# TensorE's attention as a loop with a register count over pairs of token blocks, with two V slots, x normalised by ScalarE and transposed two blocks at a time

## The reference

```python
xn = rms_norm(x)                                  # x * rsqrt(mean(x*x) + 1e-6)
qkv = xn @ w_qkv.T                                # w_qkv: 3072 x 128
q, k, v = split, 16 heads of 64
q, k = apply_rope(q, cos, sin), apply_rope(k, cos, sin)
attn = where(0 <= q_pos - k_pos <= 32, q @ k.T / 8, -1e9)
out = softmax(attn) @ v
y = out @ w_out.T                                 # back to 128 channels
```

## Time and profile before

| | us |
|---|---|
| median of 3 runs | 500.16 |
| lowest, highest | 496.52, 503.5 |
| the profiled execution's own time | 501.18 |
| its span | 499.3 |

### The profile page before, as it was taken

One profiled execution on the slowest core, in us unless ns is written; L12 is line 12 of the kernel. 1 busy time (PEld: TensorE's weight loads), 2 busy tenths in 40 slices (PEclk: granted clock), 3 DMA queues, 4 the chain that ended last, 5 costly groups with the idle time before them and its releaser, 6 DMA issues.

```text
span 499.3 us, 16604 instructions
## 1 busy us (share of the span) xinstructions
PE 401.6 (80%) x6608; PEld 353.5 (71%) x6608; DVE 312.4 (63%) x1554; ACT 255.7 (51%) x643; POOL 171.0 (34%) x196
## 2 busy tenths in 40 slices
PE   2786899879988999888899832999995669999940
PEld 2675899779987899877577632998984446777830
DVE  1676877767877788676816848222128851788855
ACT  4145666446565566564544820454401464679446
POOL 2465343624463434444344501200008770000004
PEclk9997999999999999998999985899997975999865
DMA  6456456536656566752020043000000000000002
GB/s 221 124 129 165 99 147 147 146 93 177 156 142 160 135 147 150 187 122 64 4 84 1 1 95 83 12 1 1 1 0 1 1 0 1 1 2 2 1 2 84
DMA packets 30925, 38.58 MB, mean 77 GB/s; under 512 B 8640, under 2 KB 22080, under 8 KB 30848
## 3 DMA queue, kind: packets, MB, share of 16 engines
q1 hardware_dynamic: 30272, 36.47, 29.5%
q10 hardware_dynamic: 576, 1.05, 0.7%
HBM read 8.93 MB, written 3.28 MB: 24 GB/s over the span
## 4 chain that ended last, share of the span: by engine, by line
PE 56%; DVE 13%; SPq 11%; issue 6%; DMA 5%; ACT 5%; POOL 5%; POOLq 0%; ACTq 0%; DVEq 0%
PE QK L557 6%; SPq L464 6%; PE VY L630 4%; PE O L608 3%; PE S L584 3%; PE O L699 3%; PE QK L889 3%; PE PT L594 2%; PE QK L763 2%; PE O L771 2%; PE PT L617 2%; PE QK L869 2%; PE S L680 2%; POOL qk L1539 2%; DVE unread_tests L1219 1%
## 5 line engine op out<-in xcount | busy, mean ns | idle before, releaser
L1539 POOL TENSOR_TENSOR qk<-t_cos,t_swap 128x512 f32<-128x512 f32 x64 | 80.6, 1280 | 100.9 <-DMA t_swap<-t_sin 96.9
L1308 ACT ACTIVATE probs<-probs,negative_max 128x64 f32<-128x64 f32 x256 | 68.0, 338 | 46.8 <-DVE negative_max L960 46.7
L951 DVE TENSOR_TENSOR t_cos<-QK,cos 128x512 f32<-128x512 f32 x64 | 43.9, 686 | 33.0 <-POOL qk L1539 19.3
L960 DVE CUSTOM_DVE_ANT_0 probs<-S,masks 128x64 f32<-128x64 f32 x256 | 39.4, 219 | 11.7 <-PE S L584 11.4
L951 DVE TENSOR_TENSOR t_sin<-QK,sin 128x512 f32<-128x512 f32 x64 | 43.6, 681 | 0.0
L557 PE MATMUL QK<-xnT,wq 128*128 128x128 f32 x256 | 36.0, 286 | 1.8 <-DVE t_sin L951 1.1
L1578 POOL TENSOR_TENSOR rstd<-var_eps,minus_half 128x4 f32<-128x4 f32 x24 | 25.2, 1050 | 33.7 <-DVE var_eps L1004 29.0
L608 PE MATMUL O<-v_before,probsT 64*32 64x65 f32 x1024 | 29.2, 226 | 9.1 <-issue 9.1
L1329 ACT COPY oT<-PT 128x512 f32<-128x512 f32 x32 | 18.7, 585 | 32.9 <-PE PT L617 32.9
L630 PE MATMUL VY<-wo,oT 128*128 128x128 f32 x256 | 34.9, 280 | 0.7 <-ACT oT L1329 0.7
L557 PE MATMUL QK<-xnT,wk 128*128 128x128 f32 x256 | 35.0, 281 | 0.1
(11 more groups left out here) (272 smaller groups left out, 1058.6 us busy)
## 6 DMA issues: line engine op xcount, KB each, us to landing
t_swap<-t_sin SPq DMA_DIRECT2D x124, 128.0 KB
v_before<-v_own SPq DMA_DIRECT2D x32, 132.0 KB
v_before<-v_own SPq DMA_DIRECT2D x62, 66.0 KB
late_tile<-late_weights SPq DMA_DIRECT2D x7, 189.0 KB
x_sb<-x SPq DMA_DIRECT2D x4, 256.0 KB, 4.1
inverse_dram<-invT SPq DMA_DIRECT2D x1, 1024.0 KB, 5.1
gram_dram<-gram SPq DMA_DIRECT2D x4, 256.0 KB, 2.3
invT<-inverse_dram SPq DMA_DIRECT2D x4, 256.0 KB, 4.9
```

Of the source, the lines that this page charges most:

```text
L951: last = nc.vector.tensor_tensor(dst[:, u % G, PAIRS * j:PAIRS * j + PAIRS], QK[j][:].rearrange("p (m t) -> p m t", m=PAIRS), table[:, tok ...
L960: last = nc.vector.tensor_tensor_reduce(out=probs[:, u % G, m, e, :], in0=S[:, e, m, :], in1=masks[:, min(u // G, 1), :], scale=-1.0, scal ...
L1308: last = nc.scalar.activation(probs[:, u % G, m, e, :], probs[:, u % G, m, e, :], ACT.Exp, scale=-1.0, bias=negative_max[:, u % G, e, m:m ...
L1539: nc.gpsimd.tensor_tensor(qk[:, h, c, WINDOW:WINDOW + P], t_cos[:, h, c], t_swap[:, h, c], ALU.add).then_inc(rope_done, 1)
```

## The change

TensorE's program for the steps u = 4 to 27 becomes one loop, `pe.Fori(1, NP - 1)`, that runs six times over a body of four steps (PAIR_STEPS = 4, two blocks of 128 tokens). The first four steps and the last seven stay unrolled. In the loop all counts of semaphores and the place of xnT are computed from the loop's register. Because the body has to address the same tiles in every pass:

- v_own has two slots instead of three, xn two blocks instead of 16, and xv_high and xv_low two instead of 16. keep_v(b) now waits for move_v(b-1)
- x is transposed two blocks at a time, seven times in steps 0, 4, ..., 24 behind project_v, and once ahead of the loop over steps; instead of four blocks at a time
- x is normalised by ScalarE (pairs of blocks) and no longer by VectorE; xnT is kept, staged and split per block or pair
- the squares go to a tile of their own; squares of the third and fourth group stay in ScalarE's steps 8 and 16, at their end; GpSimd's inverse root of the second group moves from ahead of unit 2 to ahead of unit 3
- the waits of a function are put in another order, and a separate nop stands behind the waits of scores and of attend

```diff
-    V_SLOTS = 3
+    PAIR_STEPS = 2 * G
+    NP = UNITS // PAIR_STEPS
+    V_SLOTS = 2
-    XT_STEP = {UG * q - 6: q for q in range(1, TG)}
...
-            def project_qk(u):
+            def project_qk(i, k):
+                u, h = PAIR_STEPS * i + k, k % G
                 for j, w in enumerate((wq, wk)):
-                    wait(pe, rope_products_done, 2 * (u - 1) + j + 1)
+                    wait(pe, rope_products_done, 2 * u + j - 1)
                     for m in range(PAIRS):
-                        last = nc.tensor.matmul(QK[j][...], w[:, f], xnT[:, block_of(u)], start=True, stop=True)
+                        last = nc.tensor.matmul(QK[j][...], w[:, f], xnT[:, bass.ts(2 * i + k // G, P)], start=True, stop=True)
...
+            def scores(i, k):
+                u, h = PAIR_STEPS * i + k, k % G
+                wait(pe, max_done, 2 * u)
                 pe.wait_ge(rope_done, 2 * u + 2)
-                wait(pe, max_done, 2 * u)
+                pe.nop(nofuse=True)
...
+            def project_out(i, k):
                 wait(pe, r1_done, u)
+                pe.wait_ge(v_kept, u + 5 if not static(i) else min(u + 5, UNITS))
+                pe.wait_ge(oT_done, u + 1)
...
+            def transpose_x(i):
+                if not static(i) or i > 0:
+                    pe.wait_ge(oT_done, PAIR_STEPS * i - 1)
+                pe.wait_ge(x_normalised, i + 2)
+                for j in range(2):
+                    last = nc.tensor.transpose(PT[:, j * P:(j + 1) * P], xn[:, j, :], ident[:])
                 last.then_inc(xT_ps, 1)
...
+            for k in range(PAIR_STEPS):
+                step(0, k)
+            with pe.Fori(1, NP - 1) as i:
+                for k in range(PAIR_STEPS):
+                    step(i, k)
+            for u in range(UNITS - PAIR_STEPS, UNITS + 3):
+                step(u // PAIR_STEPS, u % PAIR_STEPS)
...
                 if b >= V_SLOTS:
                     act.wait_ge(o_ps, G * (b - V_SLOTS + 1))
-                    act.wait_ge(v_moved[b % 2], 96 * ((b - 2) // 2 + 1) - 32 * (1 - b % 2))
+                    act.wait_ge(v_moved[(b - 1) % 2], 96 * ((b + 1) // 2) - 32 * (b % 2))
...
+            def stage_x(b):
+                act.wait_ge(xT_kept, b // 2 + 1)
+                wait(act, v_ps, G * b - G)
+                own = xnT[:, P * b:P * b + P]
+                nc.scalar.copy(xv_high[:, b % 2, 0:P], own)
+                nc.scalar.copy(xv_high[:, b % 2, P:P + D], own[:, 0:D]).then_inc(xv_staged, 1)
+
+            def normalise_x(p):
+                act.wait_ge(rms_done, p // 2 + 1)
+                wait(act, xT_ps, p)
+                for n in range(2):
+                    last = nc.scalar.mul(xn[:, n, :], x_sb[:, 2 * p + n, :], rms[:, 2 * p + n:2 * p + n + 1])
+                last.then_inc(x_normalised, 1)
...
+                if u % PAIR_STEPS == 0 and u // PAIR_STEPS < NP - 1:
+                    keep_xnT(u // PAIR_STEPS + 1)
+                if u % 2 == 1 and u + 3 < UNITS:
+                    stage_x((u + 3) // G)
+                if u % PAIR_STEPS == 2 and u // PAIR_STEPS + 2 < NP:
+                    normalise_x(u // PAIR_STEPS + 2)
+                if u in (UG, 2 * UG):
+                    squares(u // UG + 1)
...
-                if u in XT_STEP:
-                    q = XT_STEP[u]
+                if u in (3, UG + 2, 2 * UG + 2):
+                    q = u // UG + 1
                     inverse_rms(q + 1, GB * q, GB * q + GB)
```

More of the change, by code:

```diff
@@ L600, in attend @@
                 pe.wait_ge(probsT_done, u + 1)
-                pe.wait_ge(v_moved[b % 2], 96 * (b // 2 + 1) - 32 * (1 - b % 2))
                 wait(pe, o_kept, u)
+                pe.wait_ge(v_moved[slot], 96 * pairs + 96 - 32 * (1 - slot))
+                pe.nop(nofuse=True)
                 for m in range(PAIRS):
-                    for i in range(P // WINDOW):
+                    for w in range(P // WINDOW):
                         for e in range(2):
[L606 to L610, removed]
+                            r = slice(D * (e ^ (w // 2)), D * (e ^ (w // 2)) + D)
+                            v = v_own[r, slot, e] if w % 2 else v_before[r, slot, e]
+                            last = nc.tensor.matmul(O_ps[WINDOW * w:WINDOW * w + WINDOW, e, m, 0:D + 1],
+                                                    probsT[r, h, m, WINDOW * w:WINDOW * w + WINDOW],
+                                                    v[:, PAIRS * h + m, 0:D + 1], start=True, stop=True)
@@ new lines, in step @@
+            def step(i, k):
+                u = PAIR_STEPS * i + k
+                if not static(i) or u < UNITS:
+                    scores(i, k)
+                if not static(i) or 2 <= u < UNITS + 2:
+                    attend(i, k - 2)
+                if not static(i) or 1 <= u <= UNITS:
+                    transpose_probs(i, k - 1)
+                if not static(i) or u >= 3:
+                    project_out(i, k - 3)
+                if not static(i) or u + 3 < UNITS:
+                    project_qk(i, k + 3)
+                if not static(i) or 2 <= u < UNITS + 2:
+                    transpose_out(i, k - 2)
+                if not static(i) or u + 2 < UNITS:
+                    project_v(i, k + 2)
+                if k == 0 and (not static(i) or i < NP - 1):
+                    transpose_x(i)
@@ L1037, in _ @@
                 rope_products(u)
-            split_x(0)
+            for b in range(2):
+                split_x(b)
             dve.wait_ge(ld_rope[1], 32)
@@ L1347, in _ @@
                 nc.scalar.mul(half(wq, h), half(wq, h), SCALE).then_inc(wq_scaled, 1)
+            normalise_x(0)
             keep_xnT(0)
-            act.wait_ge(xT_kept, 1)
-            stage_x(0)
+            for b in range(2):
+                stage_x(b)
             act.wait_ge(ld_wv, 16)
```

144 lines of the change are left out of this document (51 added, 93 removed).

## The result

| | before | after |
|---|---|---|
| median, us | 501.83 (4 runs) | 527.0 (4 runs) |
| lowest, highest | 496.52, 503.52 | 526.46, 528.25 |
| span of the profiled execution | 499.3 | 526.5 |
| from VY of step 3 to VY of step 29 | 171.0 | 202.8 |
| ahead of VY of step 3 | 47.7 | 47.5 |

After against before is 1.056, with a 95% interval of 1.051 to 1.061; it compares the fast runs of each kernel, so it is not quite the quotient of the medians. The loss lies where the prediction put it, but is more than three times as large there: +31.8 us where +9.5 were forecast.

The account below looks back on a forecast made before the run. With two V slots, a ring through keep_v, SP's queue and move_v sets the pace, not TensorE. Thirteen rings of 13.0 us plus extras give 180.5 (+9.5), the head -2, net +7.5: forecast 508.5 us, range 501 to 526.

Parts of the forecast that it names:

- the bare ring: Two-step cycle from odd-step VY through rope products, swap_halves, move_v and keep_v to the next: 13.0 us a pair undisturbed.
- the late squares: GpSimd waits twice for ScalarE's squares, delaying the rope products of unit 12 and again later: 1.0 us each, 2.0 together.
- SP's extras: Issues between swap and move (late_tile pieces, rope loads, kv_bias, level_mask): 8.5 us; fetches in the last ring: 1.0.
- the registers: Some 17 register-based waits a step in TensorE's loop: 0.2 to 0.4 us a step expected, at most 1.7.
- the first term: From VY of an odd step through QK to the end of VectorE's rope products: 4.5 us a pair.
- the landing: From the end of move_v's last issue until its data in v_before release keep_v: 1.6 us, ends 1.3 and 1.9.
- the head: Everything ahead of VY of step 3: that VY comes at about 45.5 instead of 47.68 us, so -2.
- what follows: Everything behind VY of step 29: carried over unchanged.
- the middle: From VY of step 3 to VY of step 29, 13 rings: 180.5 us instead of 171.0, +9.5.
- Refetching each pass: Rival: TensorE's code blocks are fetched again on each pass, long SP issues stay: +14, 522.5 us; chance 0.22.
- Register work over the slack: Rival: register work on TensorE's sequencer exceeds 0.9 us a step: priced at 516 us, 527 at full bound; chance 0.15.
- The hidden move: Rival: keep_v's copy finds the move landed, TensorE sets the pace: 486.5 us, 494 with registers; chance 0.07.

Follow-up runs that it names:

- early tails: Changed kernel with the two transfers of move_v that read the older slot issued ahead of the next swap, keep_v waiting for them alone: 492.7 us, ratio 0.991.
- attend ahead of scores: Kernel with early tails, with attend(u-2) issued ahead of scores(u) in TensorE's step: 487.1 us, ratio 0.975.

## Why the prediction was wrong, and where it was right

**Right: the mechanism and its place.** The wait of keep_v, SP's ten issues, VY as the place where TensorE stands, the bare ring (13.7 against 13.6) and the late squares (2.8 against 2.0) are as forecast; SP's extras (12.0 against 9.5) nearly. So are the loop's resident body with 26 packets, the end of the stalls in O, the registers (an even step takes 6.15 us instead of 5.85), and issues of 0.60 us in the mean. One name was wrong: the older slot is what the move reads as `last`, not as `own`. The number did not depend on it, but with the right name the prediction could have seen that only two of the six transfers had to be waited for, which is the remedy.

**Wrong, the step that failed most: the first term, 4.5 us from VY to the rope products.** It measured 71.6 us over the 13 rings instead of 58.5. I took it from an example at the upper clock and carried it through all of them. But the same sum says that TensorE idles 1 to 2 us in each ring, and the example has no idle time ahead of VY. The trace of before could have warned: PE idled there for 3.9 us until 41.3, and the granted clock was 0.51 from 39.8 to 46.7 us. It was no sure sign, since a stall of O of 3.5 us, until 103.1, left the clock at 1.00. The lower clock adds 9.7 us to the term. Of the seven stretches at the lower level between 45 and 260 us, six stand behind idle stretches ahead of VY (1.8 to 5.6 us), one behind a stall of O of 2.6. With the loop written out, idle matmuls show it: 6.1 us a ring falls to 4.5, and the time by 11 us.

The Trainium skill's page "TensorE: Matmul & The Clock Gate" (HAM oscillation — how this bites in real kernels) describes just this loop of waiting for data, losing the clock and starting each round slow. The traces agree: 2.05 and 1.92 us for eight matmuls behind the wait at 47.5, 1.13 and 1.06 behind the shorter one at 145.9.

**Wrong: the landing, 1.6 us.** Undisturbed it is 1.5, and my bounds of 1.3 and 1.9 held for seven rings. In the others it took 2.2 to 4.4 us. Two stand behind rope tables (3.9 and 2.8; shown by moving the loads). In the first, with 4.4, keep_v waited 4.07 us for O and not for the move, and O had stalled for 2.6 us in the loop's first pass, until 2.9 us after a packet of code had begun. In ring 3, with 2.3, ScalarE was still at the squares (until 96.67) and copied at once behind them, at 96.85. The causes of two with 2.2 and 2.6 stay open. One reason for my bounds was wrong: the first two transfers of a move carry 132 KB, more than the 128 of a swap's; the last four carry 66. Over 13 rings +8.3 us. I had counted the rope loads by their issue, 1.1 us each, and not by what they do to the transfers behind them in the queue.

**Wrong: the head, -2.** With three slots the x work gives more, 6.1 us (VY of step 3 at 41.6). With two, the first keep_v of block 2 waits 6.10 us for the move of block 1, and VY waits for it. The prediction had this wait, but let the move start 1.3 us earlier than before, at 38.3, with issues of 3.69 us in all. It started at 40.55, behind two issues of 1.3 us and the rope loads, and took 4.76 us, since its last issue took 1.65. Timeline of ACT, kernel after:

```profile
46.82 0.59 ACT L1331 COPY v_own<-VY 128x512 f32<-128x512 f32 x1 [6.10 <-DMA v_before<-v_own]
```

VY comes at 47.5, and 0.2 us of the gain is left.

**Carried over, and changed: what follows.** Behind VY of step 29 the kernel takes 4.4 us less. I did not follow this up, and its cause stays open: it is 276.2 us with the loop written out too, but with early tails 274.0 with the loop and 280.5 without.

**The sum.** +31.8, -0.2 and -4.4 make the +27.2 between the spans. The difference to the forecast of +9.5 for the middle is 22.3: clock 9.7, landing 8.3, SP's extras 2.5, squares 0.8, and 1.0 of small gaps.

**The rivals.** Refetching each pass fell with 26 packets; its 522.5 us lay near the result for a wrong reason. Of the Trainium skill, "Runtime: NRT & Kernel Launch" (Instruction fetch mechanics), the statement on a taken branch is not what this trace shows, and the buffer of 128 KiB for TensorE is in accord with it: after the first pass one packet comes in the loop. Register work over the slack fell: 0.3 us a step, at the middle of the 0.2 to 0.4; with the loop written out undisturbed steps take 5.97 us, so that 0.1 of it belongs to the new order of waits. The hidden move fell for the change as made, and is what the early tails bring about. That their 492.7 lies within the 486.5 to 494 worked out for it is luck: the rival put the gain into the 24 steps, and there the early tails gained nothing (171.9 against 171.0); attend ahead of scores did (165.8).

## What to carry to other kernels

When a buffer is cut from three slots to two, write down which transfers really read the slot that comes free, and let the writer wait for those alone, issued as early as their data allow. When a new wait makes TensorE idle in each round, price the work behind it at the lower clock too, and put that price into the ring, because it feeds itself. A transfer on the path costs its issue and its landing, and here the landing was later when tables had been issued just ahead of it on the same queue.

## What the runs showed that I had not expected

- A loop of some 1,330 matmuls and weight loads with its waits on TensorE is run six times with its code fetched once: 26 packets against 53. It was worth 25 us with the ring (552.7 against 527.0) and 17 without it (509.9 against 492.7). The fetches cost twice, as stalls of TensorE in the middle of O and as longer DMA issues on SP, 0.70 against 0.60 us in the mean.
- Register work on TensorE is cheap: the operations take 32 to 46 ns, a satisfied wait 51, and a step is 0.3 us longer, new order of waits included.
- Work without use can pay: in the kernel with the loop written out, 12 idle matmuls a pair kept the granted clock at its upper level behind each VY and took 11 us off (541.6 against 552.7).
- A transfer between two tiles in SBUF landed 1.5 us after its issue ended, and 2.8 to 3.9 us after it when the rope tables had been issued just ahead.
